# Flamingo block on one core: the row maxima of the attention scores taken from high parts alone, the two heads of a pair in the two halves of TensorE's rows

## The reference

```python
x = x + tanh(g_xattn) * xattn(ctx_1024, layernorm(x), ln1, ln2, Wq, Wkv, Wo)
x = x + tanh(g_ffn) * ffn(layernorm(x), router, experts, conv, shared)

# xattn, for each of 16 batches and 16 heads of 64 columns:
q = l @ Wq                              # 256 rows of queries
k, v = split(concat([ctx, l]) @ Wkv)    # 77 + 256 = 333 rows of keys and values
w = softmax((q * scale) @ (k * scale).T)
out = (w @ v) @ Wo
```

## Time and profile before

| | us |
|---|---|
| median of 3 runs | 1470.83 |
| lowest and highest run | 1468.44, 1477.56 |
| span of the profiled execution | 1465.2 |

### The profile page before, as it was taken

How to read it: one execution, slowest core, us unless ns; L and a number is a source line. 1 busy time by engine, 2 the same in 40 slices (tenths; PEclk the granted TensorE clock), 3 DMA queues, 4 the chain that set the end, 5 groups by cost and what they waited for, 6 DMA issues and landing times. The chain is left out here.

```text
span 1465.2 us, 28802 instructions
## 1 busy us (share of the span) xinstructions
PE 1283.1 (88%) x8634; PEld 1054.8 (72%) x8635; DVE 1065.3 (73%) x2360; ACT 794.3 (54%) x1631; POOL 625.2 (43%) x702
## 2 busy tenths in 40 slices
PE   2899999999999999999999999999695528999970
PEld 1688888788778878878887888888494416777750
DVE  6788888788888878888897888878537103555546
ACT  2676777677666767767766677777342102222210
POOL 0344544345444444444444454444502770366630
PEclk9999999999999999999999999999956758999985
DMA  4411111111110111101111111110150220244457
GB/s 134 140 32 26 32 29 34 27 30 28 29 35 25 33 27 33 33 23 38 29 27 34 28 32 28 33 29 24 36 149 20 99 104 22 89 136 140 141 158 241
DMA packets 83414, 87.46 MB, mean 60 GB/s; under 512 B 12272, under 2 KB 77760, under 8 KB 83264
## 3 DMA queue, kind: packets, MB, share of 16 engines
q1 hardware_dynamic: 76064, 66.68, 16.4%
q0 software_dynamic: 6912, 18.92, 3.7%
q10 hardware_dynamic: 288, 0.00, 0.0%
HBM read 35.15 MB, written 33.63 MB: 47 GB/s over the span
## 5 line engine op out<-in xcount | busy, mean ns | idle before, releaser
L1014 POOL TENSOR_TENSOR OT_hl<-OT,OT_hl 128x256 fp32r<-128x256 f32 x128 | 93.7, 732 | 435.5 <-ACT OT_hl L1075 435.5
L1225 DVE TENSOR_REDUCE neg_max<-st 128x1 f32<-128x333 f32 x512 | 222.3, 496 | 33.9 <-PE st L1349 31.8
L1233 DVE RECIPROCAL inv_sum<-ov 128x256 f32<-128x256 f32 x128 | 223.7, 1748 | 6.6 <-PE ov L1326 6.6
L1049 ACT ACTIVATE probs<-st 128x512 f32<-128x512 f32 (+1 forms) x384 | 214.5, 593 | 9.2 <-PE st L1281 3.1
L1322 PE MATMUL ov<-probs,V 128*64 128x256 f32 (+1 forms) x1536 | 194.3, 388 | 4.2 <-DVE OT L1237 4.2
L1280 PE MATMUL st<-QS,KS 128*128 128x256 f32 (+1 forms) x768 | 193.2, 281 | 0.1
L1281 PE MATMUL st<-QS,KS 128*128 128x256 f32 (+1 forms) x768 | 192.9, 280 | 0.0
L1005 POOL TENSOR_TENSOR prob_sum<-probs 128x512 f32<-128x512 f32 x128 | 165.1, 1290 | 58.6 <-ACT probs L1049 58.6
L1067 ACT ACTIVATE KS<-pj 64x668 fp32r<-64x668 f32 x256 | 185.0, 723 | 7.7 <-PE pj L1251 5.7
L1009 POOL TENSOR_TENSOR prob_sum<-prob_sum,probs 77x512 f32<-77x512 f32 x128 | 164.7, 1287 | 10.0
L1251 PE MATMUL pj<-wkv,lT 128*128 128x512 f32 (+1 forms) x576 | 151.6, 399 | 5.8 <-DVE QS L1194 5.1
(11 more groups left out here) (172 smaller groups left out, 2301.0 us busy)
## 6 DMA issues: line engine op xcount, KB each, us to landing
QS<-QS SPq DMA_DIRECT2D x256, 64.0 KB, 2.0
slots_x<-zeros SPq DMA_DIRECT2D x80, 128.5 KB, 2.4
xs<-slots_x SPq DMA_DIRECT2D x80, 128.5 KB
yg<-routed_y SPq DMA_DIRECT2D x32, 256.0 KB, 3.6
out<-X SPq DMA_DIRECT2D x32, 128.0 KB, 3.4
stage<-in_L_xattn_Wkv SPq DMA_DIRECT2D x4, 512.0 KB, 3.5
X<-in_x SPq DMA_DIRECT2D x2, 1024.0 KB, 6.8
w_gu<-in_L_ffn_expert_gate_w SPq DMA_DIRECT2D x2, 960.0 KB, 8.6
```

The lines of the kernel that those rows point to most:

```text
L1014: pool.tensor_tensor(OT_hl[:, v, 1, :], OT[:, v, :], OT_hl[:, v, 0, :].bitcast(F32), ALU.subtract).then_inc(ot_lo, 1)
L1049: nc.scalar.activation(probs[0:kn, v, i, :], bank[0:kn, :], ACT.Exp, scale=SCALE).then_inc(free, 1)
L1225: nc.vector.tensor_reduce(neg_max[:, v, i // 2, i % 2:i % 2 + 1], bank[:, 0:SKV], AX.X, ALU.max, negate=True).then_inc(free, 1)
L1233: nc.vector.reciprocal(inv_sum[:, v, :], ov[:, SQ:2 * SQ]).then_inc(inv_ready, 1)
```

## The change

The four approximate-score matmuls take plane 0 of `QS` and plane 1 of `KS`, and of both only the 64 rows in which the head's high parts lie: rows 0 to 63 for head 0, rows 64 to 127 for head 1. So they leave out K's low part. They run in another order, heads alternating (head 0 and head 1 for the first 128 queries, then both for the second), and the column of `neg_max` that VectorE writes follows. They no longer read the second copy of Q's high part, so the wait for `q_dup` goes from them to the first true scores of the pair, two steps later. The transfers themselves stay.

```diff
@@ VectorE, step @@
-                        nc.vector.tensor_reduce(neg_max[:, v, i // 2, i % 2:i % 2 + 1], bank[:, 0:SKV], AX.X,
+                        nc.vector.tensor_reduce(neg_max[:, v, i % 2, i // 2:i // 2 + 1], bank[:, 0:SKV], AX.X,
                                                 ALU.max, negate=True).then_inc(free, 1)
@@ TensorE, scores(i) @@
                     if i == 0:
+                        turn = PAIRS // RING
+                        pe.wait_ge(q_dup[m], 32 * (turn * bb + (u - LAG_S) // RING + 1))
                         _, _, mfree, mvalue = filled("M", PAIRS, bb, u - LAG_S)
@@ TensorE, step @@
                 if has(LAG_APX):
                     m = (u - LAG_APX) % RING
-                    turn = PAIRS // RING
-                    pe.wait_ge(q_dup[m], 32 * (turn * bb + (u - LAG_APX) // RING + 1))
                     _, _, kfree, kvalue = filled("K", PAIRS, bb, u - LAG_APX)
                     pe.wait_ge(kfree, kvalue + 1)
                     for i in range(4):
-                        head, qt = i // 2, i % 2
+                        head, qt = i % 2, i // 2
+                        own = slice(head * HALF, (head + 1) * HALF)
                         _, bank, free, value = filled("A", 4 * PAIRS, bb, 4 * (u - LAG_APX) + i)
                         pe.wait_ge(free, value)
-                        mm(bank[:, 0:SKVE], QS[:, m, head, 0, qt * P:(qt + 1) * P], KS[:, m, head, 0, :],
+                        mm(bank[:, 0:SKVE], QS[own, m, head, 0, qt * P:(qt + 1) * P], KS[own, m, head, 1, :],
                            start=True, stop=True).then_inc(st_full, 1)
```

## The result

| | us |
|---|---|
| median before (4 runs) | 1469.67 |
| median after (4 runs) | 1484.0 (1480.09 to 1484.98) |
| ratio, 95% interval | 1.0087 (1.0056 to 1.0118) |
| spans of the profiled executions | 1465.2 before, 1482.8 after |

The account below looks back on a forecast made before the run. TensorE's stream was taken to bound the attention; +0.098 us in each of 128 steps gave +12.5 us, so span 1465.2 to 1477.7 and median 1470.8 + 12.5, less a little relief, 1483 us. Range 1430 to 1492.

Parts of the forecast that it names:

- Two halves of the rows run side by side: Approximate scores on TensorE: heads 0 and 1 overlap in their own rows, 0.31 us in place of 0.61 a step.
- A change of division drains TensorE, 0.095 each: TensorE going into and out of the row-half stretch: each change of the array's division costs 0.095 us.
- The first load behind a drain lies open, 0.11 for 128 columns: Weight loads at both ends of the stretch: not hidden under a matmul, 0.11 us for 128 columns, 0.065 for 77.
- Sum +0.098 us a step, +12.5 us: The whole stretch on TensorE: 0.712 us against 0.614 a step, over 128 steps.
- VectorE's later start costs nothing: VectorE's first two reductions get their banks together, moved by 0.1 us; cost 0 while it has 16% idle.
- The moved wait costs nothing: TensorE's wait for `q_dup`, two steps later: nothing waited for the copies before, nothing will; cost 0.
- The clock stays at 1.00: TensorE's granted clock: holds despite the idle times at weight loads in each step, so no cost.
- rival 1: Row halves need no change of division, loads stay hidden: -39 us, 1432 us; chance 0.19.
- 2 (one drain only): Only one of the two changes costs, or loads hide in both gaps: -13 us, 1458 us; chance 0.10.
- 3 (loads one after another): Both halves' weight loads share one path: +34 us, 1505; without any matmul overlap +51 us, 1522; chance 0.15.
- 4: Whole rows are driven all the same, no overlap, no change of division: 0.61 us stays, 1471 us; chance 0.05.

Follow-up runs that it names:

- e3: The changed kernel with all four approximate-score matmuls in rows 0 to 63, so the second half is unused; 1524.06 us, ratio 1.0325 to the kernel before.
- e6: The kernel before, whole rows kept, with the approximate scores moved ahead of the two transposes; ratio 1.0095.
- e11: The changed kernel with one pair of approximate scores ahead of the transposes and one behind; ratio 1.0173 to the kernel before.
- e1: The kernel before with only the change's other edits (alternating heads, VectorE's column, moved q_dup wait), whole rows kept; ratio 1.0002.
- e12: Changed kernel: approximate scores ahead of transposes, awaiting K's high part; ScalarE exponentials mostly earlier, VectorE layer norm split, POOL's second deviation later; 1470.25 us, ratio 0.9973 to before.
- e9: Changed kernel: approximate scores ahead of transposes, awaiting K's high part; ScalarE exponentials mostly earlier, VectorE's layer norm behind the pair's normalisation; ratio 1.0508 to before.
- e2: The changed kernel with the four approximate matmuls in the old order, head 0 twice, then head 1 twice; 1490.78 us, ratio 1.0098 to before.

## Why the prediction was right

The steps of the sum, as they were put, against what was measured:

- *Two halves of the rows run side by side.* Predicted 0.31 for four matmuls. Shown by e3: without the second half 0.30 us a step more. Pairs start 0.001 to 0.007 us apart.
- *A change of division drains TensorE, 0.095 each.* Measured 0.09 in and 0.09 out. Shown by e3 (drain without a second half), e6 (no division added, none of it) and e11 (one change and load more, +0.20 a step). The rule of the Trainium skill, TensorEngine Tiling (Array Packing), Key Properties, holds for row halves in this kernel as for column halves.
- *The first load behind a drain lies open, 0.11 for 128 columns.* Measured 0.107 to 0.109. Shown by itself in e6, where it costs about 0.10 us a step without a change of division more.
- *Sum +0.098 us a step, +12.5 us.* That is a mean over steps that load 128 columns behind the stretch (where the same terms give +0.109) and steps that load 77. The step shown above is of the first kind and measures +0.085; the two steps of the second kind are 0.03 to 0.04 us longer than before. Over a batch the steps, less what VectorE's lateness adds (next item), grow by 0.60 us, 0.075 a step: 9.6 us. So the forecast was 2.9 us too dear by small errors of one sign: the stretch before was taken as 0.614 and is 0.617, the two pairs as 0.313 and are 0.305, and each drain and load a few thousandths too long.
- *VectorE's later start costs nothing.* Wrong in one step of eight. There TensorE's K projection waits for the bank that VectorE frees at L1150, behind its four reductions; the first approximate scores end about 0.2 us later than before, and the projection begins 0.78 us behind the first true score instead of 0.64 (undisturbed 0.47). That is 0.14 x 16 = 2.2 us. Where scores were moved ahead, this step became shorter by 0.21 than before (e6) or by 0.29 than after the change (e11).
- *The moved wait costs nothing.* Right (e1).
- *The clock stays at 1.00.* It does through the steps, with their idle times of 0.2 to 0.4 us. Behind the loop's returns it doesn't, and the prediction has no term for that: one fall in the profile before, four after, about 4.5 us.

Together a batch takes 0.74 us more, 11.9 us in all. The steps at the loop's returns took 15.7 us over normal ones in the profile before (one fall of the clock), 17.7 in e1 (two) and about 20 after (four). So the profiled span grew by 17.6 us, to 1482.8, where 1477.7 had been forecast. How much of that is the change's doing can't be told from one profile each: beside e12 the kernel before itself took from 1467.74 us (mean granted clock 0.936) to 1483.81 us (0.928). The median's +14.3 us, with an interval of 8 to 17, agrees with 11.9 alone and with more.

That the number fell within 1 us of the median is partly luck: the stretch was forecast 2.9 us too dear, the VectorE step 2.2 too cheap, and the clock behind the returns was left out. Two slips of the working changed nothing: rival 1's step comes to 7.5 us, not 7.6, and with the change at 0.12 and the load at 0.13 its own terms reach +0.19 a step, not +0.17.

The rivals: 1 (no drain) fell to the rows above; 2 (one drain only) would be 0.73 us from transpose to projection, it is 0.81 with the load behind it still open; 3 (loads one after another) fell to e3's busy times; 4 to both.

## What to carry to other kernels

In this kernel row halves of TensorE pay a drain and an open weight load at each end of the stretch, about 0.2 us with 128 columns of weights (column halves pay the same drain and a shorter load), so count how many matmul streams a stretch saves: four matmuls of 334 columns save 0.31 us and lose by two ends, eight win. Put stretches of different divisions next to each other, and behind each a matmul with few weight columns, so that a drain that is there anyway serves both. And where an engine's order is moved, look for who stands behind it in a third engine: POOL's wait in e9 cost 5% for the 0.6 us a batch that was sought. When two profiles of a loop are compared, look at the granted clock behind its returns before the difference is put down to the change.

## What the runs showed that was not expected

- Matmuls of different row halves overtake each other: with heads in turn the third of four started 0.007 us behind the first and 0.25 ahead of the second (e2). A semaphore that counts finished matmuls then no longer says which bank is full. If the matmuls also end in this order (their ends are modelled in the trace), VectorE's count of two in e2 stands for banks one and three, and nothing in the program guards the second. No run shows harm from it.
- A drain of 0.09 us comes with every change between whole, column halves and row halves, whether both halves are used or one, and a transpose with 2 columns of weights counts as whole: between transposes and whole-array matmuls there is none.
- The loop's five returns cost TensorE 2.0 to 3.5 us of idle time each, and where its granted clock falls behind them 1.5 to 3 us more. The length of the idle time alone doesn't tell whether it falls: after the change it fell behind 2.3 us and stayed behind 2.5.
